# Linear attention, SwiGLU and two LayerNorms on 8 cores: x tiles loaded one step earlier, and a second pair of staging buffers for the int32 weights

## The chip, the cores and the metric

The kernel runs on all 8 cores of one Trainium2 chip. The batch of 16 sequences is split, two to a core, and the cores do not talk to each other. The time is that of the slowest core, in microseconds (us), from the first to the last instruction of the launch with what lies around it.

## The reference

With x of 16 x 2048 x 1024 in float32, layer 0 is

```python
q = elu(x @ Wq.T) + 1          # 16 heads of 64
k = elu(x @ Wk.T) + 1
v = x @ Wv.T
KV  = einsum('bshd,bshe->bhde', k, v)          # one 64 x 64 matrix per head and sequence
out = einsum('bshd,bhde->bshe', q, KV)
out = out / (einsum('bshd,bhd->bsh', q, k.sum(axis=1)) + 1e-6)
x = layernorm(x + out @ Wo.T)
h = silu(x @ (w_gate/127).T) * (x @ (w_up/127).T)      # hidden 3072, int32 weights
x = layernorm(x + h @ (w_down/127).T)
```

## The kernel before

**Two phases of attention.** A core holds 2 sequences of 2048 tokens. Since KV needs all tokens of a sequence, `phase1` goes first over the 16 token tiles of 128: it computes k and v of a tile (lines 535 and 549, 16 matmuls each), then the per-head products of the tile before (`emit_kv`, line 484), which VectorE adds up in `kv_acc`. Then 4 tiles of 512 tokens follow, each with a `phase2` (q, attention output, Wo, LayerNorm 1) and a `phase3` (gate and up projections, 24 slabs `m` of 128 hidden units, lines 1112 and 1125, with `silu` on ScalarE, line 1144, and the product into `h_fm` on VectorE, line 1152). The down projection (line 718) of a 512-token tile is done within `phase2` of the next one. The order of the tiles in `phase1` starts at tile 4 and ends with tiles 0 to 3, so that `xT` then holds the first 512 tokens for `phase2`.

**How x comes in.** `load_x_ld` (line 439) loads 128 tokens in float32 into one of two buffers `x_f32`, `load_x_cast` (line 448) turns them into bf16 on ScalarE, and `load_x_tp` (line 457) transposes them by DMA into a quarter of `xT`. In `phase1` all three for tile u+1 are in the body of tile u: load and cast at its head, the transpose at its end. `phase2` does the same for the next 512 tokens of the same sequence in the steps of `px`; for the last 512 tokens of a sequence (`next_x` is None) it does nothing, and the first tile of the next sequence is loaded at the head of the next `phase1`.

**Weights.** In the first sequence they come in while the work runs: Wk and Wv directly (`load_pair_direct`, through four staging buffers, of which two are the `x_f32` buffers), then, four jobs per tile of `phase1` (`drain_w_jobs`), Wq and Wo in float32 (cast on ScalarE, line 383, written back to HBM as bf16), and the 24 slabs of w_down in int32 (cast on VectorE and GpSimd into `wd_buf`). The gate and up slabs are loaded by `load_slab`. In the first `phase3` of the kernel (`first_tile`) each is an int32 image of 512 KB, loaded into a staging buffer `stg_i32` (line 1021), cast into `wgu[:, gi, m % 4, :]` (line 1033: gate on VectorE, up on GpSimd) and written to a bf16 copy in HBM (line 1048) that all later tiles read (lines 1062 and 1070). Slab m+4 is asked for in the body of slab m. Gate images always go through `outb[:, 0]` and up images through `outb[:, 1]`. The gate cast is emitted one slab later (`defer_vec`), ahead of that slab's `h_fm` on VectorE.

**What sets the order.** There is no scheduler: each engine executes its instructions in the order of the Python code. All DMAs, loads, stores and transposes alike, are issued by SyncE (SP) in that one order, each with its waits ahead of it; a `Track` for each buffer gives the waits (the readers and the writer before). So one DMA that waits holds back all behind it.

Of the kernel before, what the change touches and what calls it, by code (L numbers as in the profile page):

```python
# [9 lines left out]
I32 = mybir.dt.int32  # L10
# [4 lines left out]
SEQ = 2048  # L15
NSEQ = 2
D = 1024
# [165 lines left out]
def build_program(n_seq=NSEQ, n_tiles=NTILE // NSEQ, stop_after=None):  # L183
# [17 lines left out]
    with contextlib.ExitStack() as ctx:  # L201
# [75 lines left out]
        tr_silu = [Track() for _ in range(2)]  # L277
        tr_stgi = [Track() for _ in range(4)]
        tr_stgb = [Track() for _ in range(4)]
# [11 lines left out]
        for r in range(2):  # L291
# [4 lines left out]
                   wgu[:, 0, :, :].rearrange("p a b -> p (a b)").bitcast(I32)[:, 0:D],  # L296
                   wgu[:, 1, :, :].rearrange("p a b -> p (a b)").bitcast(I32)[:, 0:D]]
        stg_bf = [h_fm[:, 2 * i:2 * i + 2, :].rearrange("p a b -> p (a b)")
# [145 lines left out]
        def load_x_cast(ent, tq):  # L444
            ld, xr = ent
            ct = P.op("scalar",
                      lambda e, xr=xr, tq=tq:
                      e.activation(x_bf[:, tq, :], x_f32[:, xr, :], AF.Copy),  # L448
                      waits=[ld, tr_xbf[tq].begin_write()])
            tr_x[xr].add_reader(ct)  # L450
            tr_xbf[tq].end_write(ct)
            return ct
# [17 lines left out]

        def phase1(s, first):
            NCH = SEQ // 128
            pend = {}

            def emit_kv(u):
# [23 lines left out]
                else:  # L499
# [8 lines left out]
            order = [(u + CPT) % NCH for u in range(NCH)]  # L508
            cts = {0: load_x_cast(load_x_ld(s * SEQ + order[0] * 128),
                                  order[0] % CPT)}  # L510
            load_x_tp(cts.pop(0), order[0] % CPT)
            if first:
                load_pair_direct("wk", "wv")
            for u in range(NCH):
                if u + 1 < NCH:
                    cts[u + 1] = load_x_cast(
                        load_x_ld(s * SEQ + order[u + 1] * 128),
                        order[u + 1] % CPT)
                tq = order[u] % CPT
# [9 lines left out]
                for j in range(NJ):  # L529
                    for hl in range(2):  # L530
# [10 lines left out]
                            inc=last)  # L541
                bend(kbk, tok)
                for j in range(NJ):
                    for hl in range(2):
# [47 lines left out]
                pend[u] = (kr, kvr, t_k, t_v)  # L592
                if u + 1 < NCH:
                    load_x_tp(cts.pop(u + 1), order[u + 1] % CPT)

# [414 lines left out]
        def load_slab(m, first_tile=False, both_gp=False, defer_vec=None):  # L1010
# [4 lines left out]
            if first_tile:  # L1015
                for gi, (mat, img) in enumerate((("wg", wi_imgs["wgi"]),
                                                 ("wu", wi_imgs["wui"]))):
                    sl = (2 * m + gi) % 2
                    ld = P.dma(f"w3i{sl}",
                               lambda sy, img=img, m=m, sl=sl:  # L1020
                               sy.dma_start(stg_i32[sl], img[m]),
                               waits=[tr_stgi[sl].begin_write(),
                                      tr_outb[sl].begin_write()],
                               eng=BULKQ)
                    tr_stgi[sl].end_write(ld)
                    tr_outb[sl].end_write(ld)

                    def mk_ct(gi=gi, r=r, sl=sl, ld=ld, m=m, mat=mat,
                              both_gp=both_gp):
                        eng = "gpsimd" if (both_gp or gi == 1) else "vector"  # L1030
# [6 lines left out]
                        tr_stgi[sl].add_reader(ct)  # L1037
                        tr_outb[sl].add_reader(ct)
                        tr_wgu[gi][r].end_write(ct)
# [130 lines left out]
        for s in range(n_seq):  # L1170
            phase1(s, first=(s == 0))
            if stop_after == "P1":
# [5 lines left out]
            for g in range(n_tiles):  # L1178
                tidx = s * n_tiles + g
                sl3 = CPT - 1 + (tidx % 2)  # L1180
                nx = (s * SEQ + (g + 1) * TILE) if g + 1 < n_tiles else None
                fj = None
# [78 lines left out]
```

How the kernel before makes its waits and increments, by code:

```python
        def closure(eng, fn=fn, real_waits=real_waits, tok=tok, sem=sem):  # L128
            for s, v in real_waits:
                eng.wait_ge(s, v)
            inst = fn(eng)
            if tok is not None:
                inst.then_inc(sem, 1)
# [15 lines left out]
        def closure(e, fn=fn, real_waits=real_waits, sem=sem):  # L149
            for s, v in real_waits:
                e.wait_ge(s, v)
            fn(e).then_inc(sem, 16)
# [7 lines left out]
        def closure(eng, real_waits=real_waits):  # L160
            for s, v in real_waits:
                eng.wait_ge(s, v)
```

## Time and profile before

| | |
|---|---|
| median of the runs, us | 1936.92 |
| the runs, us | 1872.54 and 2001.31 |
| the profiled execution's own time, us | 1867.76 |
| its span on the slowest core (core 1), us | 1866.2 |
| spans of the 8 cores, us | 1850.5 to 1866.2 |
| TensorE busy, us (share of the span) | 1570.0 (84%) |
| ScalarE, VectorE busy, us | 545.9, 519.3 |
| bytes moved by DMA in core 1 | 255.28 MB, mean 137 GB/s |

All rows below are of the profiled execution, core 1; times in them count from the start of its span. The first sequence ends at 968 us. Engines: PE is TensorE, ACT ScalarE, DVE VectorE, POOL GpSimd, SPq the issue of a DMA by SyncE. A busy time of PE can overlap the start of the next group by a few tenths of a microsecond. In the windows view, the DMA share is the time that DMA packets took, as a share of 16 engines; packets that overlap can take it over 1.

### The profile page before, as it was taken

The numbers are of one execution on the slowest core, as the hardware profiler recorded it, in microseconds if no ns is written. First come the engines' busy times: TensorE is split into PE (matmuls) and PEld (weight loads), VectorE is DVE, ScalarE is ACT, GpSimd is POOL, SyncE is SP. The second block draws the span as 40 slices with busy tenths as digits, with TensorE's granted clock in tenths as the row PEclk, the third lists the DMA queues.
The fourth block names the chain that finished last, engine by engine and source line by source line (L and its number), as shares of the span: only waits on it lengthen the run. The fifth ranks groups of instructions, "written<-read, shape, count | busy, mean of one in ns | idle before, by whom it ended". The sixth has DMA issues, their size and how long they took to land.

```text
span 1866.2 us, 23063 instructions; the slowest of 8 cores (1850.5 to 1866.2 us)
## 1 busy us (share of the span) xinstructions
PE 1570.0 (84%) x7424; PEld 686.1 (37%) x7424; DVE 519.3 (28%) x979; ACT 545.9 (29%) x801; POOL 42.6 (2%) x44
## 2 busy tenths in 40 slices
PE   2677755766999899989888888899899999989998
PEld 0233322322444344434333333344344344434443
DVE  1142342123321332232113333312331332233111
ACT  2432213111342152224113331432252234114213
POOL 0010001110000000000000000000000000000000
PEclk9798977989999999999899998899899999999999
DMA  7999447885444245413653433355145334512431
GB/s 230 250 300 261 119 132 178 252 250 169 113 130 153 63 108 156 138 29 96 204 152 88 99 73 114 91 153 147 47 120 163 101 95 134 154 53 68 138 106 45
DMA packets 213236, 255.28 MB, mean 137 GB/s; under 512 B 136320, under 2 KB 136320, under 8 KB 212096
## 3 DMA queue, kind: packets, MB, share of 16 engines
q1 hardware_dynamic: 213120, 253.81, 47.9%
q8 instruction: 64, 1.05, 0.2%
q14 instruction: 52, 0.43, 0.1%
HBM read 184.55 MB, written 37.75 MB: 119 GB/s over the span
## 4 chain that ended last, share of the span: by engine, by line
PE 67%; DMA 13%; DVE 8%; ACT 6%; issue 4%; SPq 1%; DVEq 0%; ACTq 0%; POOL 0%; POOLq 0%
PE ps_c L718 18%; PE ps_a L1112 16%; PE ps_b L1125 15%; PE ps_b L924 5%; DMA outb<-wgi 5%; PE ps_a L535 3%; PE ps_b L549 2%; PE ps_a L549 2%; PE ps_b L535 2%; DVE t L812 2%; ACT texp L819 2%; DVE q_fm L826 2%; PE ps_a L799 2%; DMA res<-wo 1%; DMA x_f<-wv 1%
## 5 line engine op out<-in xcount | busy, mean ns | idle before, releaser
L1125 PE MATMUL ps_b<-ln1T,wgu 128*128 128x512 bf16 x1536 | 372.5, 386 | 32.3 <-DVE h_fm L1152 32.3
L1112 PE MATMUL ps_a<-ln1T,wgu 128*128 128x512 bf16 x1536 | 368.6, 383 | 26.9 <-DMA ln1T<-ln_bf 9.4
L718 PE MATMUL ps_c<-wd_buf,h_fm 128*128 128x512 bf16 x1536 | 355.7, 392 | 0.0
L1144 ACT ACTIVATE silu_b<-ps_a,consts 128x512 bf16<-128x512 f32 x192 | 131.1, 687 | 538.9 <-PE ps_a L1112 460.3
L1152 DVE SCALAR_TENSOR_TENSOR h_fm<-ps_b,silu_b 128x512 bf16<-128x512 f32 x192 | 131.9, 691 | 487.6 <-PE ps_b L1125 454.6
L1125 PEld LDWEIGHTS ps_b<-ln1T,wgu 128*128 128x128 bf16 x1536 | 151.3, 99 | 223.6 <-issue 51.0
L1112 PEld LDWEIGHTS ps_a<-ln1T,wgu 128*128 128x128 bf16 x1536 | 151.2, 99 | 215.3 <-issue 40.0
L718 PEld LDWEIGHTS ps_c<-wd_buf,h_fm 128*128 128x128 bf16 x1536 | 153.5, 101 | 186.9 <-issue 21.4
L924 PE MATMUL ps_b<-wpair,attnT 128*128 128x512 bf16 x512 | 134.1, 422 | 30.3 <-DVE res L948 16.7
L622 ACT ACTIVATE texp<-res 128x1024 bf16<-128x1024 f32 x64 | 67.3, 1051 | 299.7 <-DVE res L741 238.1
L799 PE MATMUL ps_a<-xT,wpair 128*128 128x512 bf16 x512 | 126.3, 396 | 31.9 <-DVE q_fm L826 27.0
L535 PE MATMUL ps_a<-wpair,xT 128*128 128x512 bf16 x256 | 70.3, 430 | 70.9 <-ACT wpair L413 34.5
L535 PE MATMUL ps_b<-wpair,xT 128*128 128x512 bf16 x256 | 64.4, 409 | 34.8 <-ACT v_tm L572 19.4
L924 PEld LDWEIGHTS ps_b<-wpair,attnT 128*128 128x128 bf16 x512 | 53.0, 107 | 101.5 <-issue 59.2
L799 PEld LDWEIGHTS ps_a<-xT,wpair 128*128 128x128 bf16 x512 | 48.5, 100 | 108.2 <-issue 62.6
L819 ACT ACTIVATE texp<-t 128x512 bf16<-128x512 bf16 x64 | 40.3, 629 | 124.1 <-DVE t L812 124.0
L847 PE MATMUL ps_a<-kvbd,q_fm 128*128 128x130 bf16 x256 | 29.3, 237 | 48.9 <-DVE attn_bf L889 30.4
L448 ACT ACTIVATE x_bf<-x_f 128x1024 bf16<-128x1024 f32 x56 | 57.9, 1043 | 26.9 <-DMA x_f<-x 26.9
L535 PEld LDWEIGHTS ps_a<-wpair,xT 128*128 128x128 bf16 x256 | 25.4, 105 | 109.6 <-issue 89.5
L826 DVE SCALAR_TENSOR_TENSOR q_fm<-ps_a,texp 128x512 bf16<-128x512 f32 x64 | 44.3, 692 | 64.0 <-ACT texp L819 64.0
L741 DVE SCALAR_TENSOR_TENSOR res<-ps_c,ln_bf 128x1024 f32<-128x1024 f32 x32 | 39.0, 1219 | 82.8 <-PE ps_c L718 79.9
L549 PE MATMUL ps_b<-wpair,xT 128*128 128x512 bf16 x256 | 58.8, 383 | 0.6
(59 smaller groups left out, 800.8 us busy)
## 6 DMA issues: line engine op xcount, KB each, us to landing
wgu<-scr_wg SPq DMA_DIRECT2D x168, 256.0 KB, 2.7
wgu<-scr_wu SPq DMA_DIRECT2D x168, 256.0 KB, 2.6
x_f<-x SPq DMA_DIRECT2D x56, 512.0 KB, 4.1
out<-outb SPq DMA_DIRECT2D x32, 512.0 KB, 2.7
outb<-wgi SPq DMA_DIRECT2D x24, 512.0 KB, 5.0
outb<-wui SPq DMA_DIRECT2D x24, 512.0 KB, 5.3
outb<-wdi SPq DMA_DIRECT2D x12, 512.0 KB, 7.6
wgu<-wdi SPq DMA_DIRECT2D x12, 512.0 KB, 8.6
```

The costliest lines, as they stand in the source:

```text
L535: t.matmul(kps[:, hl * 512:(hl + 1) * 512], xT[:, j, tq * 128:(tq + 1) * 128], wpair[:, 0, j, hl * 512:(hl + 1) * 512], start=(j == 0), st ...
L549: t.matmul(vps[:, hl * 512:(hl + 1) * 512], xT[:, j, tq * 128:(tq + 1) * 128], wpair[:, 1, j, hl * 512:(hl + 1) * 512], start=(j == 0), st ...
L622: e.activation(texp[:], res[:, rr, :], AF.Square, accum_out=stats[:, sl, 1:2]),
L718: t.matmul(d_view[:, pr, hl * 512:(hl + 1) * 512], h_fm[:, hm, sc * 128:(sc + 1) * 128], wd_buf[:, hm, hl * 512:(hl + 1) * 512], start=(hm ...
L799: t.matmul(ps_a[:, (i % 2) * 512:(i % 2 + 1) * 512], wpair[:, 0, j, i * 128:(i + 1) * 128], xT[:, j, :], start=(j == 0), stop=(j == NJ - 1)),
L819: lambda e: e.activation(texp[:, 0:TILE], t1[:, 0:TILE], AF.Exp),
L826: v.scalar_tensor_tensor(q_fm[:, i, :], ps_a[:, (i % 2) * 512:(i % 2 + 1) * 512], 0.0, texp[:, 0:TILE], ALU.max, ALU.add),
L924: t.matmul(ps_b[:, hl * 512:(hl + 1) * 512], attnT[:, tc, e_, :], wpair[:, 1, e_, hl * 512:(hl + 1) * 512], start=(e_ == 0), stop=(e_ == N ...
L1112: t.matmul(ps_a[:, (m % 2) * 512:(m % 2 + 1) * 512], wgu[:, 0, r, j * 128:(j + 1) * 128], ln1T[:, j, :], start=(j == 0), stop=(j == NJ - 1)),
L1125: t.matmul(ps_b[:, (m % 2) * 512:(m % 2 + 1) * 512], wgu[:, 1, r, j * 128:(j + 1) * 128], ln1T[:, j, :], start=(j == 0), stop=(j == NJ - 1)),
L1144: e.activation(silu_b[:, m % 2, :], ps_a[:, (m % 2) * 512:(m % 2 + 1) * 512], AF.Silu, scale=consts[:, 2:3]),
L1152: v.scalar_tensor_tensor(h_fm[:, m, :], ps_b[:, (m % 2) * 512:(m % 2 + 1) * 512], INV127, silu_b[:, m % 2, :], ALU.mult, ALU.mult),
```

## The change

Three things are changed.

1. `phase1` loads x two tiles ahead. The loads of tiles 0 and 1 stand at its head, the load of tile u+2 and the transpose of tile u+1 stand between the k and v matmuls of tile u, and the cast of tile u+1 stays at the head of tile u.
2. `phase2` of the last 512 tokens of the first sequence loads, casts and transposes tiles 4 to 7 of the second sequence (the first four in the order of `phase1`), and `phase1` of the second sequence then starts its loads at the fifth.
3. In the first `phase3`, slabs with odd m from 5 on are staged in `attnT` (two halves, for gate and up) instead of `outb`. `attnT` is idle in `phase3`.

```diff
@@ phase1
-            cts = {0: load_x_cast(load_x_ld(s * SEQ + order[0] * 128),
-                                  order[0] % CPT)}
-            load_x_tp(cts.pop(0), order[0] % CPT)
+            start_i = 4 if pre_x else 0
+            cts = {}
+            lds = {}
+
+            def p1_ld(i):
+                if start_i <= i < NCH:
+                    lds[i] = load_x_ld(s * SEQ + order[i] * 128)
+
+            def p1_cast(i):
+                if i in lds:
+                    cts[i] = load_x_cast(lds.pop(i), order[i] % CPT)
+
+            def p1_tp(i):
+                if i in cts:
+                    load_x_tp(cts.pop(i), order[i] % CPT)
+
+            p1_ld(0)
+            p1_ld(1)
+            p1_cast(0)
+            p1_tp(0)
             if first:
+                p1_cast(1)
                 load_pair_direct("wk", "wv")
             for u in range(NCH):
-                if u + 1 < NCH:
-                    cts[u + 1] = load_x_cast(
-                        load_x_ld(s * SEQ + order[u + 1] * 128),
-                        order[u + 1] % CPT)
+                p1_cast(u + 1)
...
                 bend(kbk, tok)
+                p1_ld(u + 2)
+                p1_tp(u + 1)
...
-                if u + 1 < NCH:
-                    load_x_tp(cts.pop(u + 1), order[u + 1] % CPT)
@@ load_slab
-                    sl = (2 * m + gi) % 2
+                    sl = gi + (4 if (m >= 4 and m % 2 == 1) else 0)
+                    if sl >= 4:
+                        alias = [tr_attnT[(sl - 4) * 2], tr_attnT[(sl - 4) * 2 + 1]]
+                    else:
+                        alias = [tr_outb[sl]]
                     ld = P.dma(f"w3i{sl}",
                                lambda sy, img=img, m=m, sl=sl:
                                sy.dma_start(stg_i32[sl], img[m]),
-                               waits=[tr_stgi[sl].begin_write(),
-                                      tr_outb[sl].begin_write()],
+                               waits=[tr_stgi[sl].begin_write()]
+                                     + [t.begin_write() for t in alias],
                                eng=BULKQ)
@@ the calls
-            phase1(s, first=(s == 0))
+            phase1(s, first=(s == 0), pre_x=(s > 0))
...
-                nx = (s * SEQ + (g + 1) * TILE) if g + 1 < n_tiles else None
+                if g + 1 < n_tiles:
+                    nx = s * SEQ + (g + 1) * TILE
+                elif s + 1 < n_seq:
+                    nx = (s + 1) * SEQ + CPT * 128
+                else:
+                    nx = None
```

**SP in the first `phase3`.** These are the first rows of the queue of SyncE there before the change: `wgi` and `wui` are the int32 images of gate and up, `scr_wg` and `scr_wu` their bf16 copies in HBM; a semaphore in brackets is what a row waits for.

```order
L1021 DMA outb<-wgi 128x1024 [waits sem_gpsimd,dsl_w3i0]
L1021 DMA outb<-wui 128x1024 [waits sem_gpsimd,dsl_w3i1]
L1048 DMA scr_wg<-wgu 128x1024 [waits dsl_scw0]
L1048 DMA scr_wu<-wgu 128x1024 [waits dsl_scw1]
L1021 DMA outb<-wgi 128x1024 [waits sem_vector,dsl_w3i0]
L1021 DMA outb<-wui 128x1024 [waits sem_gpsimd,dsl_w3i1]
L1048 DMA scr_wu<-wgu 128x1024 [waits dsl_scw1]
L1048 DMA scr_wg<-wgu 128x1024 [waits dsl_scw0]
L1021 DMA outb<-wgi 128x1024 [waits sem_vector,dsl_w3i0]
L1021 DMA outb<-wui 128x1024 [waits sem_gpsimd,dsl_w3i1]
```

And the same place after the change:

```order
L1042 DMA outb<-wgi 128x1024 [waits sem_gpsimd,dsl_w3i0]
L1042 DMA outb<-wui 128x1024 [waits sem_gpsimd,dsl_w3i1]
L1071 DMA scr_wg<-wgu 128x1024 [waits dsl_scw0]
L1071 DMA scr_wu<-wgu 128x1024 [waits dsl_scw1]
L1042 DMA attnT<-wgi 128x1024 [waits sem_tensor]
L1042 DMA attnT<-wui 128x1024 [waits sem_tensor,dsl_at0,dsl_at1]
L1071 DMA scr_wu<-wgu 128x1024 [waits sem_gpsimd,dsl_scw1]
L1071 DMA scr_wg<-wgu 128x1024 [waits sem_vector,dsl_scw0]
L1042 DMA outb<-wgi 128x1024 [waits dsl_w3i0]
L1042 DMA outb<-wui 128x1024 [waits dsl_w3i1]
```

Before, the load of each slab waited for the casts of the slab just ahead of it (`sem_vector`, `sem_gpsimd`), and the stores of that slab came behind. Now the loads of two slabs stand ahead of the stores that wait for the casts of the first of them, and a load itself waits for no cast that its queue has not already passed.

**SP from the last `phase3` of the first sequence into the second `phase1`.** The first two rows are the last gate and up slabs loaded in advance for the next tile; then come the x tiles of the second sequence. Before:

```order
L1062 DMA wgu<-scr_wg 128x1024 [waits sem_tensor,dsl_wg1]
L1070 DMA wgu<-scr_wu 128x1024 [waits sem_tensor,dsl_wu1]
L439 DMA x_f<-x 128x1024 [waits dsl_x0]
L457 DMA_TRANSPOSE xT<-x_bf 128x8x128 [waits sem_scalar,dsl_xt0]
L439 DMA x_f<-x 128x1024 [waits dsl_x1]
L457 DMA_TRANSPOSE xT<-x_bf 128x8x128 [waits sem_scalar,dsl_xt1]
```

After:

```order
L1085 DMA wgu<-scr_wg 128x1024 [waits sem_tensor,dsl_wg1]
L1093 DMA wgu<-scr_wu 128x1024 [waits sem_tensor,dsl_wu1]
L441 DMA x_f<-x 128x1024 [waits dsl_x0]
L441 DMA x_f<-x 128x1024 [waits dsl_x1]
L459 DMA_TRANSPOSE xT<-x_bf 128x8x128 [waits sem_tensor,sem_scalar,dsl_xt0]
L441 DMA x_f<-x 128x1024 [waits dsl_x0]
```

The first transpose here was that of the sequence's first tile in the order of `phase1`; now it is that of its fifth, and the first four stand some 50 rows further up, in `phase2`.

**SP in the first `phase1`.** One tile of x among the loads of w_down (`wdi`), before:

```order
L457 DMA_TRANSPOSE xT<-x_bf 128x8x128 [waits sem_tensor,sem_scalar,dsl_xt1]
L439 DMA x_f<-x 128x1024 [waits dsl_x0]
L342 DMA outb<-wdi 128x1024 [waits sem_vector,dsl_wi0]
L342 DMA outb<-wdi 128x1024 [waits sem_gpsimd,dsl_wi1]
L342 DMA wgu<-wdi 128x1024 [waits sem_vector,dsl_wi2]
L342 DMA wgu<-wdi 128x1024 [waits sem_gpsimd,dsl_wi3]
```

After:

```order
L441 DMA x_f<-x 128x1024 [waits dsl_x0]
L459 DMA_TRANSPOSE xT<-x_bf 128x8x128 [waits sem_tensor,sem_scalar,dsl_xt1]
L344 DMA outb<-wdi 128x1024 [waits sem_vector,dsl_wi0]
L344 DMA outb<-wdi 128x1024 [waits sem_gpsimd,dsl_wi1]
L344 DMA wgu<-wdi 128x1024 [waits sem_vector,dsl_wi2]
L344 DMA wgu<-wdi 128x1024 [waits sem_gpsimd,dsl_wi3]
```

The load of the tile after next now stands ahead of the transpose instead of behind it; the four weight loads keep their place.

## Rows read from the trace of the kernel before

**Rows 1.** The page: busy shares in 40 slices of the span.
```profile
PE   2677755766999899989888888899899999989998
DMA  7999447885444245413653433355145334512431
```

**Rows 2.** Timeline of PE, around the first phase3 and the one after it.
```profile
312.57 3.57 PE L1112 MATMUL ps_a<-ln1T,wgu 128*128 128x512 bf16 x8 [9.37 <-DMA ln1T<-ln_bf]
...
443.12 3.62 PE L799 MATMUL ps_a<-xT,wpair 128*128 128x512 bf16 x16
...
529.86 1.89 PE L1112 MATMUL ps_a<-ln1T,wgu 128*128 128x512 bf16 x8
...
614.16 3.62 PE L799 MATMUL ps_a<-xT,wpair 128*128 128x512 bf16 x16
```

**Rows 3.** Waits in the first phase3, 313 to 443 us: waiter <- releaser, total, times, longest.
```profile
DVE wgu L1033 <- DMA outb<-wgi: 89.5, 19, 6.6
PE ps_b L1125 <- DVE h_fm L1152: 32.3, 15, 4.3
```

**Rows 4.** Timeline of SP and DVE in the first phase3.
```profile
313.34 0.46 SPq L1021 DMA_DIRECT2D outb<-wgi  x1
...
351.25 0.33 SPq L1021 DMA_DIRECT2D outb<-wgi  x1
...
357.24 0.69 DVE L1033 CAST wgu<-outb 128x1024 bf16<-128x1024 int32 x1 [5.52 <-DMA outb<-wgi]
358.07 0.33 SPq L1021 DMA_DIRECT2D outb<-wgi  x1
...
435.83 0.69 DVE L1033 CAST wgu<-outb 128x1024 bf16<-128x1024 int32 x1 [3.27 <-DMA outb<-wgi]
```

**Rows 5.** Windows: per stretch busy times, granted clock, DMA share, GB/s.
```profile
core 1: us, PE busy (x) PEld busy (x) DVE busy (x) ACT busy (x) POOL busy (x), PEclk, DMA share, GB/s
0.00:17.00 17.00, 0.00 (x0) 0.00 (x0) 0.27 (x5) 3.40 (x3) 0.20 (x4) 1.00 0.50 120
42.00:54.00 12.00, 5.00 (x18) 1.86 (x16) 1.58 (x2) 6.41 (x7) 0.00 (x0) 0.88 0.86 261
54.00:101.00 47.00, 29.06 (x144) 11.79 (x144) 9.17 (x9) 20.87 (x21) 0.00 (x0) 0.79 0.94 256
112.00:165.00 53.00, 45.69 (x269) 19.98 (x270) 24.33 (x27) 17.37 (x17) 10.97 (x10) 0.97 1.09 314
313.34:435.83 122.49, 90.18 (x352) 36.18 (x351) 25.35 (x40) 16.40 (x23) 19.98 (x19) 0.89 0.84 252
886.00:896.00 10.00, 1.85 (x9) 0.64 (x7) 0.69 (x1) 0.69 (x1) 0.00 (x0) 0.74 0.96 350
```

**Rows 6.** Timeline of PE and SP from the first sequence into the second.
```profile
968.57 0.36 SPq L439 DMA_DIRECT2D x_f<-x  x1
...
976.63 5.06 PE L535 MATMUL ps_a<-wpair,xT 128*128 128x512 bf16 x16 [8.62 <-DMA xT<-x_bf]
981.53 3.62 PE L549 MATMUL ps_b<-wpair,xT 128*128 128x512 bf16 x16
```

**Rows 7.** Timeline of PE: phase2 of the fourth 512 tokens, its first group and the one behind it.
```profile
785.77 3.62 PE L799 MATMUL ps_a<-xT,wpair 128*128 128x512 bf16 x16
...
872.45 1.89 PE L1112 MATMUL ps_a<-ln1T,wgu 128*128 128x512 bf16 x8
```

**Rows 8.** The xT tile in the first 235 us, and SP and PE in the first phase1.
```profile
  DMA xT<-x_bf: 19.3, 5
...
7.72 1.33 SPq L457 DMA_TRANSPOSE xT<-x_bf  x1
...
40.04 0.33 SPq L439 DMA_DIRECT2D x_f<-x  x1
...
161.87 8.70 SPq L457 DMA_TRANSPOSE xT<-x_bf  x1
...
175.58 6.21 PE L535 MATMUL ps_b<-wpair,xT 128*128 128x512 bf16 x16 [9.29 <-DMA xT<-x_bf]
```

More of the change, by code:

```diff
@@ L277, in build_program @@
         tr_silu = [Track() for _ in range(2)]
-        tr_stgi = [Track() for _ in range(4)]
+        tr_stgi = [Track() for _ in range(6)]
         tr_stgb = [Track() for _ in range(4)]
@@ L296, in build_program @@
                    wgu[:, 0, :, :].rearrange("p a b -> p (a b)").bitcast(I32)[:, 0:D],
-                   wgu[:, 1, :, :].rearrange("p a b -> p (a b)").bitcast(I32)[:, 0:D]]
+                   wgu[:, 1, :, :].rearrange("p a b -> p (a b)").bitcast(I32)[:, 0:D],
+                   attnT[:, 0:2, :, :].rearrange("p a b c -> p (a b c)").bitcast(I32),
+                   attnT[:, 2:4, :, :].rearrange("p a b c -> p (a b c)").bitcast(I32)]
         stg_bf = [h_fm[:, 2 * i:2 * i + 2, :].rearrange("p a b -> p (a b)")
@@ L469, in dbg_dump, with phase1 @@
             P.sync_wait([tk])
-        def phase1(s, first):
+        def phase1(s, first, pre_x=False):
             NCH = SEQ // 128
@@ L1021, in load_slab @@
                                sy.dma_start(stg_i32[sl], img[m]),
-                               waits=[tr_stgi[sl].begin_write(),
-                                      tr_outb[sl].begin_write()],
+                               waits=[tr_stgi[sl].begin_write()]
+                                     + [t.begin_write() for t in alias],
                                eng=BULKQ)
                     tr_stgi[sl].end_write(ld)
-                    tr_outb[sl].end_write(ld)
+                    for t in alias:
+                        t.end_write(ld)
                     def mk_ct(gi=gi, r=r, sl=sl, ld=ld, m=m, mat=mat,
-                              both_gp=both_gp):
+                              both_gp=both_gp, alias=alias):
                         eng = "gpsimd" if (both_gp or gi == 1) else "vector"
@@ L1037, in mk_ct @@
                         tr_stgi[sl].add_reader(ct)
-                        tr_outb[sl].add_reader(ct)
+                        for t in alias:
+                            t.add_reader(ct)
                         tr_wgu[gi][r].end_write(ct)
```

## The prediction

> **What bounds the kernel now.** I read the slices of the page first [rows 1]. The reader is to see three kinds of stretch: in the first four slices TensorE is busy 2 to 7 tenths while the DMA engines are at 7 to 9; in slices 7 and 8 (counting from 0, 326 to 420 us) TensorE is at 6 and 7 and DMA at 8; from slice 10 on TensorE is at 8 and 9 nearly everywhere and DMA at half or less. So TensorE is the bound outside the first 445 us, and there only a stall of its own can be won; before that the DMAs are.
>
> The second view is the timeline of TensorE, which gives each stage its length [rows 2]. The first `phase3` runs from 312.57 to 443.12 us, 130.6 us; the next one does the same matmuls in 614.16 - 529.86 = 84.3 us, 3.5 us a slab. The difference of 46 us is what the int32 slabs cost. The third view, the waits of that stretch, tells how [rows 3]: VectorE waits 89.5 us in 19 waits for gate images to land, and since its queue is in order the product `h_fm` stands behind that cast; TensorE then waits 32.3 us for `h_fm`. The timeline shows the cycle [rows 4]: the load issued at 351.25 us is cast at 357.24, 6.0 us later, and only then, at 358.07, is the next load issued, because there is one staging buffer for gate images. The windows view says that this leaves DMA at 252 GB/s and a share of 0.84 [rows 5].
>
> The last stall that the change speaks of is at the seam of the two sequences [rows 6]: x is asked for only at 968.57 us, and TensorE, done with `phase3`, stands still for 8.62 us.
>
> **Part 1: the staging buffers.** In the changed queue of SP the loads of slab m+1 are out before the casts of slab m are waited for, so two slabs are in flight. A load at the head then waits for no cast that SP hasn't passed, and nothing new is queued behind a wait: the store of the up slab, which now is what SP stands at, was behind such a wait before. The two casts need slab m-4's matmuls to be done, which TensorE, slowed to the DMA's pace, is. The buffer `attnT` was read last by the Wo matmuls before 312 us, so its first load finds it free.
>
> The stretch then ends with the stream of bytes. From the first gate load at 313.34 to the landing of the last at 435.83 us are 122.5 us [rows 4]. In the queue up to that landing are 20 gate and 19 up images of 0.524 MB (20.45 MB) and 38 stores of 0.262 MB (9.96 MB), 30.4 MB. Bounds for the rate, with these bytes:
> - 256 GB/s, as between 54 and 101 us, where loads, stores and transposes are mixed and the share is 0.94 [rows 5]: 118.8 us
> - 314 GB/s, as between 112 and 165 us, mostly int32 loads, share 1.09 [rows 5]: 96.8 us
> - between them the stretch itself, 252 GB/s at a share of 0.84, which is 300 GB/s at 1.00 [rows 5]: 101.3 us.
>
> I take 300, as it is the same mixture of packets, and add 1.5 us for the landing of the last image, my estimate: an image takes 6.0 us now from issue to cast, of which it and the up image beside it are 3.5 us at 300 GB/s, and a part of the rest is paid each time. The part gives 122.5 - 102.8 = 19.7 us, with bounds of 2.2 and 24.2. TensorE does not become the bound: its 24 slabs at 3.5 us end at 397 us, the stream at 416. The 7.3 us from the last gate cast to the end of the stage (435.83 to 443.12) stay. Later tiles only move up: their x is there already, and their slabs are read from the copies in HBM.
>
> **Part 2: the seam.** Four tiles of x lie in `xT` before TensorE is done with `phase3`. The 8.62 us go, and with them the slow restart: the 16 matmuls behind the stall took 5.06 us against 3.62 for the same number right after [rows 6], 1.4 us. What is late next is the PSUM bank that `silu` of slab 23 reads, and that is free before TensorE arrives. 10.1 us are won. The fifth tile has the time of four others, 7.2 us of matmuls each, to come in, and is no stall. The lower bound is 8.6 us, if the restart stays slow.
>
> The price is four loads, four casts on ScalarE and four transposes more in the last `phase2` of the sequence, and behind the last two of these transposes stand an output store and the load of Wk and Wv. The `phase2` of the second 512 tokens carries just this and shows the price [rows 2, 7]: it takes 529.86 - 443.12 = 86.7 us, the last one, without it, 872.45 - 785.77 = 86.7 us. I take nothing. What hides it is the down projection of the last 128 tokens on TensorE; without that cover the Wk and Wv load would slip by the two transposes.
>
> **Part 3: the first `phase1`.** TensorE waits here for x transposes 5 times, 19.3 us in all, 9.29 of them at once at 175.58 us [rows 8], where the transpose is queued behind two stores of 2 MB. As DMA is full from 112 to 165 us, the end of that wait is set by the bytes ahead of it. The changed order puts one tile of x more (0.524 MB, 1.7 us at 300 GB/s) ahead of each transpose. In return tile 1 is loaded at the very start, where SP stands still until 7.72 us and DMA is half idle [rows 5, 8], instead of at 40.04 us: 1.7 us fewer from there on. The two cancel. What is left is idle DMA time that earlier loads may fill: 0.14 of 12 us (42 to 54 us) and 0.06 of 47 us (54 to 101 us) [rows 5], 1.7 + 2.8 = 4.5 us, since ScalarE then finds x there and comes to its weight casts sooner. I take half of it, 2.3 us won. The bounds are 6.2 us won (all of it, and the 1.7 of the start without its counterweight) and 8.5 us lost (1.7 us on each of the 5 waits). In the second `phase1` DMA has room, and swapping load and transpose costs nothing there.
>
> **The sum.** 19.7 + 10.1 + 2.3 = 32.1 us. Against the profiled execution's own time, 1867.8 us, that is 1836 us, a ratio of 0.983. The two runs shown are 1872.54 and 2001.31 us and their median, 1936.92, is only their mean; the forecast is on the scale of the lower one, which it would put at 1841.
>
> **Rivals.**
> - **The stream is not held back by buffers.** The DMA engines might already do all that this mixture of loads and stores allows. For it: 256 GB/s at 54 to 101 us is no more than the 252 of the stage [rows 5]. Against it: the share there is 0.94 and here 0.84, and transposes take part of it there. Part 1 gives 2.2 us or less, the sum is 14.6, the time 1853.
> - **The stream runs faster than 314 GB/s.** For it: between 886 and 896 us 350 GB/s flow [rows 5]. Against it: these are bf16 loads alone. At 350 the 30.4 MB take 86.9 us, 88.4 with the landing; TensorE, at 397 us, is still done earlier. Part 1 gives 34.1 us, the sum is 46.5, the time 1821. The Trainium skill, "HBM Reference", Specifications, says that each of two cores that stream at once gets about 358 GB/s; the 350 GB/s above agree, and no stretch with stores comes near. By that rule the bytes would take 84.9 us and part 1 would give 36 us, a time of about 1819.
> - **The earlier x loads fill the queue in front of the transposes (the other side).** At 161.87 us the issue of one transpose took 8.70 us, where the first took 1.33, with 4 MB of stores just ahead of it [rows 8]; SP and all that it feeds stand still meanwhile. If one more tile of x ahead of it did the same to a transpose among the w_down loads, each would cost 8.70 - 1.33 = 7.4 us. It decides from five of them on: 36.9 us against the 32.1 won, 1873 us, slower than before. Against it: of the 19.3 us that TensorE waits for x, 9.29 stand behind this one transpose, so none of the others, which have 2.6 MB of w_down and x before them, was held back as much.
>
> **How the numbers follow.** My forecast holds with a chance of 0.60, for itself from 1827 (a rate of 314 and all 6.2 us of part 3) to 1850 (a rate of 275, where part 1 gives 10.5 us, and 3 us lost in part 3). The fast stream has 0.18, the stream without gain 0.17, the full queue 0.05. The range of 8 in 10 goes from 1817 to 1866 us: below it takes in the fast stream, above it the case without gain with part 3 at its bad end (1867.8 - 2.2 - 10.1 + 8.5 = 1864). A measurement of this kernel can tell about 2% from no change, 37 us, so "faster by over 2%" is below 1830: the fast stream nearly whole, 0.16, and the quick edge of the forecast, 0.11, together 0.27. Slower by over 2% takes the full queue with more transposes than five, 0.02. Within 2% is the rest, 0.71.
>
> **What would show it.** Right: in the first `phase3` the gate loads on average 5.1 to 5.4 us apart (101 us over 19) instead of 6.4 (122.5 over 19), at 300 GB/s and a share near 1, the stage at 108 to 114 us in place of 130.6, and VectorE's waits for gate images still the largest but near 65 us. At the seam no wait of TensorE for `xT`, and its first 16 k matmuls at 3.6 us. In the first `phase1` the end of the long wait within 3 us of 175.6. Wrong: a rate that stays at 252 GB/s with two slabs in flight; a stall that comes back at the fifth tile of the second sequence; a TensorE wait for `ln1T` or for Wk and Wv in the last tile of the first sequence longer than before; issues of transposes above 3 us between 105 and 153 us.

## The result and the profile after

The changed kernel takes 1834.9 us, the median of 11 runs (1833.6 to 1931.4). In some runs, such as that of 1931.4 us, one half of the chip has a lower granted clock and the time is longer; all ratios here leave such runs out on both sides. The ratio to the kernel before is 0.9798, with a 95% interval of 0.9752 to 0.9844. Measured again beside the experiments below (e5) it was 0.9826 (0.9804 to 0.9849). The forecast was 1836 us and 0.983. The profiled execution took 1841.2 us, 26.6 less than the 1867.8 of the one before; the measured ratios stand for 32 to 38 us.

The timeline of TensorE in the changed kernel, core 1 again, the first matmuls of each stage, answers to [rows 2, 6, 7]. Columns: start in us, length in us, line, output<-inputs, shape, and in brackets the wait ahead of it.

```profile
313.23 3.57 PE L1135 MATMUL ps_a<-ln1T,wgu 128*128 128x512 bf16 x8 [9.45 <-DMA ln1T<-ln_bf]
...
426.87 3.62 PE L816 MATMUL ps_a<-xT,wpair 128*128 128x512 bf16 x16
...
513.56 1.89 PE L1135 MATMUL ps_a<-ln1T,wgu 128*128 128x512 bf16 x8
...
881.39 3.52 PE L1135 MATMUL ps_a<-ln1T,wgu 128*128 128x512 bf16 x8 [9.58 <-DMA wgu<-scr_wg]
...
952.09 3.62 PE L552 MATMUL ps_a<-wpair,xT 128*128 128x512 bf16 x16
955.55 3.62 PE L568 MATMUL ps_b<-wpair,xT 128*128 128x512 bf16 x16
```

The reader is to see three things. The first `phase3` lasts 426.87 - 313.23 = 113.6 us, where it was 130.6 [rows 2]. The `phase2` behind it is unchanged, 86.7 us. And at 952.09 us the second sequence starts without a bracket: no wait for x, and the 16 matmuls take 3.62 us instead of 5.06 [rows 6]. What is left between the sequences is the row at 881.39, a wait of 9.58 us for slab 4, which was there before (8.7 us) and which the change does not touch.

The waits of that first `phase3`, 313 to 427 us, answer to [rows 3] (waiter <- releaser, total, times, longest):

```profile
DVE wgu L1055 <- DMA attnT<-wgi: 36.3, 10, 5.8
...
DVE wgu L1055 <- DMA outb<-wgi: 31.4, 8, 5.5
PE ps_b L1148 <- DVE h_fm L1175: 21.2, 14, 3.5
```

VectorE still waits for gate images, 67.7 us in all, now for both buffers in turn; it was 89.5. TensorE's wait for `h_fm` fell from 32.3 to 21.2 us. The queue of SP in that stage answers to [rows 4]:

```profile
313.92 0.47 SPq L1042 DMA_DIRECT2D outb<-wgi  x1
...
350.64 0.40 SPq L1042 DMA_DIRECT2D attnT<-wgi  x1
...
354.67 0.33 SPq L1071 DMA_DIRECT2D scr_wu<-wgu  x1
355.15 0.33 SPq L1071 DMA_DIRECT2D scr_wg<-wgu  x1
355.58 0.39 SPq L1042 DMA_DIRECT2D outb<-wgi  x1
...
413.70 0.38 SPq L1042 DMA_DIRECT2D attnT<-wgi  x1
```

The loads into `attnT` at 350.64 and into `outb` at 355.58 are 4.9 us apart; the first was cast at 357.06:

```profile
357.06 0.69 DVE L1055 CAST wgu<-attnT 128x1024 bf16<-128x1024 int32 x1 [3.26 <-DMA attnT<-wgi]
```

So the second load went out 1.5 us before the first was used; before the change it had to go out after. Over the stage the gate loads are (413.70 - 313.92) / 19 = 5.25 us apart. The windows view of the stretch answers to the row of 313 to 436 us in [rows 5] (columns as there):

```profile
0.00:17.00 17.00, 0.00 (x0) 0.00 (x0) 0.27 (x5) 3.96 (x4) 0.20 (x4) 1.00 0.53 137
...
42.00:54.00 12.00, 7.00 (x18) 2.39 (x18) 1.84 (x2) 5.22 (x6) 0.00 (x0) 0.91 0.79 233
54.00:101.00 47.00, 29.12 (x144) 11.77 (x144) 9.17 (x9) 22.10 (x23) 0.00 (x0) 0.79 1.00 258
...
313.34:417.00 103.66, 83.55 (x344) 34.29 (x342) 25.00 (x39) 15.72 (x22) 18.72 (x18) 0.93 0.91 294
```

In the first `phase3` the DMA share rose from 0.84 to 0.91 and the rate from 252 to 294 GB/s. In the first `phase1` there is little to see: in the first 17 us the rate rose from 120 to 137 GB/s, from 42 to 54 us it fell from 261 to 233, and from 54 to 101 us the share rose from 0.94 to 1.00 while the rate went only from 256 to 258 GB/s. What TensorE waits for there has changed its name. The view of the tile `xT`, first 235 us, before:

```profile
  ACT v_tm L572: 27.8, 10
  DMA xT<-x_bf: 19.3, 5
```

and after:

```profile
  DMA xT<-x_bf: 32.3, 7
  ACT v_tm L591: 7.3, 7
  ACT texp L598: 5.8, 1
```

Before, 47.1 us of waits for ScalarE and transposes together; after, 45.4. TensorE now waits little for ScalarE and waits for the transpose instead; e3 and e8 below show that the order of the x loads does this.

### The profile page after: what moved, and what is told of

The parts are those of the page before. It is cut to its first block, busy times and chain, and to the rows that moved or that the text cites. A ratio compares the mean times of both kernels' runs of the same rounds, so it can differ in the third digit from the quotient of the medians.

```text
span 1839.6 us, 23066 instructions; the slowest of 8 cores (1815.7 to 1839.6 us)
## 1 busy us (share of the span) xinstructions
PE 1563.3 (85%) x7424; PEld 684.5 (37%) x7424; DVE 520.8 (28%) x979; ACT 544.9 (30%) x801; POOL 41.8 (2%) x44
## 4 chain that ended last, share of the span: by engine, by line
PE 67%; DMA 13%; DVE 7%; ACT 7%; issue 4%; SPq 1%; POOL 1%; DVEq 0%; ACTq 0%; POOLq 0%
PE ps_c L735 18%; PE ps_a L1135 16%; PE ps_b L1148 15%; PE ps_b L941 5%; PE ps_a L568 3%; PE ps_a L552 3%; PE ps_b L552 2%; PE ps_b L568 2%; DVE t L829 2%; ACT texp L836 2%; DMA attnT<-wui 2%; DVE q_fm L843 2%; DMA xT<-x_bf 2%; PE ps_a L816 2%; DMA scr_wu<-wgu 1%
## 5 line engine op out<-in xcount | busy, mean ns | idle before, releaser
L1148 PE MATMUL ps_b<-ln1T,wgu 128*128 128x512 bf16 x1536 | 367.7, 383 | 21.2 <-DVE h_fm L1175 21.2
L1167 ACT ACTIVATE silu_b<-ps_a,consts 128x512 bf16<-128x512 f32 x192 | 131.2, 687 | 522.2 <-PE ps_a L1135 464.6
L864 PE MATMUL ps_a<-kvbd,q_fm 128*128 128x130 bf16 x256 | 28.9, 235 | 48.9 <-DVE attn_bf L906 30.4
L504 DVE TENSOR_TENSOR kv_acc<-kv_acc,ps_c 128x520 f32<-128x520 f32 x30 | 20.9, 696 | 135.9 <-PE ps_c L486 135.9
```

The costliest lines, as they stand in the source:

```text
L1148: t.matmul(ps_b[:, (m % 2) * 512:(m % 2 + 1) * 512], wgu[:, 1, r, j * 128:(j + 1) * 128], ln1T[:, j, :], start=(j == 0), stop=(j == NJ - 1)),
L1167: e.activation(silu_b[:, m % 2, :], ps_a[:, (m % 2) * 512:(m % 2 + 1) * 512], AF.Silu, scale=consts[:, 2:3]),
```

## The experiments

Since the 8 cores of one execution differ by some microseconds, I compare stages by the median over the cores of one profiled execution: for each core, the time from the first matmul of the stage to the first of the next. The stages are the first `phase1`, the first `phase3`, the last `phase3` of the first sequence (it takes in the waits for slab 4 and, before the change, for x at the seam) and the second `phase1`. Ratios are to the kernel before, measured beside each set, with 95% intervals. The two without a ratio were run once each and are read from their profile alone; part of their result is not computed.

| kernel | ratio | phase1, 1st | phase3, 1st | phase3 at the seam | phase1, 2nd |
|---|---|---|---|---|---|
| before | 1 | 209.4 | 131.2 | 102.5 | 157.6 |
| the change | 0.9798 (0.9752 to 0.9844) | 209.1 | 112.6 | 94.7 | 155.9 |
| e1 staging only | 0.9898 (0.9872 to 0.9923) | 210.5 | 108.6 | 102.3 | 157.6 |
| e2 seam only | 0.9937 (0.9916 to 0.9959) | 208.4 | 130.5 | 94.1 | 155.9 |
| e3 order of x only | 0.9995 (0.9981 to 1.0009) | 208.1 | 129.6 | 104.3 | 157.5 |
| e4 staging and seam | 0.9839 (0.9819 to 0.9858) | 210.5 | 110.0 | 93.6 | 155.7 |
| e5 the change again | 0.9826 (0.9804 to 0.9849) | 205.5 | 108.7 | 92.8 | 155.6 |
| e6 three slabs in flight | 0.9811 (0.9794 to 0.9828) | 206.3 | 107.6 | 93.0 | 155.9 |
| e7 Wk and Wv in pieces | 0.9771 (0.9752 to 0.9789) | 207.4 | 108.4 | 84.6 | 154.8 |
| e8 transpose first | 0.9820 (0.9798 to 0.9842) | 206.1 | 111.0 | 94.1 | 155.9 |
| e9 no stores | one run, 1810.7 us | 206.9 | 85.2 | 93.9 | 156.1 |
| e10 no stores, one pair | one run, 1837.2 us | 207.6 | 114.2 | 94.6 | 156.2 |
| e11 e6 and e7 together | 0.9785 (0.9755 to 0.9815) | 207.0 | 106.0 | 84.6 | 154.7 |

### One part at a time

The first set takes the change apart. Staging alone:

```diff
-                    sl = (2 * m + gi) % 2
+                    sl = gi + (4 if (m >= 4 and m % 2 == 1) else 0)
...
-                               waits=[tr_stgi[sl].begin_write(),
-                                      tr_outb[sl].begin_write()],
+                               waits=[tr_stgi[sl].begin_write()]
+                                     + [t.begin_write() for t in alias],
```

> Only the staging of odd slabs in attnT is changed; x is loaded as before. Theory A (the parts add, each with the size seen on TensorE's timeline of core 1: 16.9 us for the first phase3, 9 to 10 for the seam, nothing for the order of the x loads): ratio to before 0.991, first phase3 113 to 115 us instead of 130.6, seam stall of 8.6 us still there. Theory B (the staging is worth more than core 1 shows, since all cores give the HBM back sooner and the other cores gain more): ratio 0.985 or lower. A rival of both, that the DMA engines had no room and the gain came from elsewhere: first phase3 128 us or more, ratio 0.998 or higher.

Measured: 0.9898 (0.9872 to 0.9923), 19 us on 1868. The wait for x at the seam is still there (9.8 us on its slowest core). The ratio is that of theory A, and its interval does not reach the 0.985 of theory B. The stage is not: 108.6 us, where theory A said 113 to 115. Over the cores it became 22.6 us shorter than before, more than core 1 had shown (16.9), so that much of theory B's argument stands. The third theory, that the gain came from elsewhere, falls.

The seam alone, with the order of `phase1` as before:

```diff
-            phase1(s, first=(s == 0))
+            phase1(s, first=(s == 0), pre_x=(s > 0))
...
+                elif s + 1 < n_seq:
+                    nx = (s + 1) * SEQ + CPT * 128
```

> Only the four x tiles of the second sequence are loaded in the last phase2 of the first; the order of loads and transposes in phase1 and the staging are as before. Theory A: ratio 0.995 (9 to 10 us), no wait of TensorE for xT at the seam, the last phase2 at 86.7 us within 0.6. Rival (the seam only moves the wait to the fifth tile, or the load of Wk and Wv slips by the two transposes): ratio 0.998 or higher, a wait of 3 us or more at the fifth tile, or one for wgu longer than 8.7 us by 2 or more.

Measured: 0.9937, 11.8 us. The timeline of TensorE at the seam on its slowest core shows no wait in front of the k matmuls of line 551:

```profile
965.91 1.89 PE L1146 MATMUL ps_b<-ln1T,wgu 128*128 128x512 bf16 x8
967.64 3.62 PE L551 MATMUL ps_a<-wpair,xT 128*128 128x512 bf16 x16
```

The wait for slab 4 is 9.43 us on that core, and between cores it differs much: 5.6 to 9.4 us here (median 7.2), 5.5 to 10.2 in the kernel before (median 6.8). So no slip of the Wk and Wv load can be seen. The rival falls.

The order of the x loads alone:

```diff
+            p1_ld(0)
+            p1_ld(1)
...
                 bend(kbk, tok)
+                p1_ld(u + 2)
+                p1_tp(u + 1)
```

> Only the x loads of phase1 are moved (load of tile u+2 ahead of the transpose of tile u+1, tile 1 loaded at the start). Theory A: ratio 1.000 within 0.001; the long wait for xT ends within 3 us of 175.6 us; TensorE's waits for xT grow and those for v_tm on ScalarE shrink by about as much. The prediction's part 3 (idle DMA time is filled): ratio 0.999, 2.3 us won. Rival (this part carries the 10 us by which the measured ratio beats the profiles): ratio 0.995 or lower. The other side: each transpose later by a tile's bytes, 1.002 to 1.005.

Measured: 0.9995 (0.9981 to 1.0009). It is no change that can be measured, neither a gain of 10 us nor the other side; the 2.3 us of the prediction (0.999) lie inside the interval too. The waits moved as expected: for `xT` 30.2 us, for `v_tm` 6.3. The long wait for `xT` ended at 173.84 us.

The two parts that do something, with the order of the x loads taken back from the change:

```diff
-                p1_ld(u + 2)
-                p1_tp(u + 1)
...
+                p1_ld(u + 1)
                 p1_cast(u + 1)
...
                 pend[u] = (kr, kvr, t_k, t_v)
+                p1_tp(u + 1)
```

> The whole change without the new order in phase1: staging and seam. Theory A: the same as the whole change within 0.001, and the sum of the first two runs. If the order of the x loads costs what the later start of the second phase1 tiles in the profile suggests (0.7 to 2.4 us), this one is faster than the whole change by 0.0005 to 0.0015. Rival (the order carries part of the gain): slower than the whole change by 0.003 or more.

Measured: 0.9839 (0.9819 to 0.9858). The sum of the first two, 1 - 0.0102 - 0.0063 = 0.9835, is the same: the parts add. Against the first 0.9798 of the whole this left 0.004 open, so the whole was run again (no edit):

> The whole change once more, with the runs of before on the same chip as the three that follow. The first set gave staging 0.9898, seam 0.9937, order 0.9995, staging and seam 0.9839; the first measurement of the whole gave 0.9798 (0.9752 to 0.9844). Theory A (the parts add): 0.983 to 0.984, so that the first value was the spread of the runs of before. Theory C (the order of the x loads is worth 0.004 beside the other two parts, though nothing alone): 0.980.

Measured: 0.9826 (0.9804 to 0.9849). That is within 0.0004 of theory A: the three parts, 0.0102 + 0.0063 + 0.0005, make 0.0170, and the whole gives 0.0174. The 0.9798 rests on runs of before that spread from 1864.9 to 1891.5 us, and its wide interval takes in 0.983.

### What holds the stream of weights

e6 adds a third pair of staging buffers and lets four stores wait instead of two, so that a third slab is asked for before SP stands at a store.

```diff
+                   q_fm[:, 0:4, :].rearrange("p a b -> p (a b)").bitcast(I32),
+                   q_fm[:, 4:8, :].rearrange("p a b -> p (a b)").bitcast(I32)]
...
-                    sl = gi + (4 if (m >= 4 and m % 2 == 1) else 0)
+                    sl = gi + (0, 4, 6)[m % 3 if m >= 4 else 0]
...
-                        while len(slab_state["st"]) > 2:
+                        while len(slab_state["st"]) > 4:
```

> The whole change plus a third pair of staging buffers (in q_fm, idle there) and four pending stores instead of two, so that the loads of three slabs are out before SP waits for a cast. Theory A (at two slabs in flight the stream of 30 MB is held by the DMA engines: share 0.91, 294 GB/s): the first phase3 shrinks by 0 to 3 us from 113.6, the rate stays below 305 GB/s, ratio to before within 0.001 of the whole change. Rival (buffers still bind, the engines could do 314 GB/s or more): phase3 at 108 us or less, ratio 0.003 better than the whole change.

Measured: 0.9811 beside 0.9826, intervals that overlap, and a first `phase3` of 107.6 us beside 108.7. The windows view of its slowest core in that stage:

```profile
308.00:405.00 97.00, 81.26 (x344) 33.90 (x342) 25.15 (x39) 15.71 (x22) 18.72 (x18) 0.94 0.94 311
```

A share of 0.94 and 311 GB/s look like a rise from the 0.91 and 294 of the changed kernel, but these are single cores. The medians over the cores, each from its first gate load of the stage to its last gate cast, are 0.92 and 314 GB/s in e5 and 0.95 and 317 here, both above the 305 I had given as the most. What is left to win by buffers is about 1 us. The rival of 108 us or less with a ratio better by 0.003 is met in the stage and missed in the ratio (0.0015); the stage had been at 108.7 already, so the step, not the level, decides, and it is small.

Two runs then separate the buffers from the bytes. They leave out the 48 stores of the bf16 copies; SP waits for the same casts in their place, and later tiles read other copies of the same size.

```diff
-                            st = P.dma(f"scw{(2 * m + gi) % 2}",
-                                       lambda sy, mat=mat, m=m, gi=gi, r=r:
-                                       sy.dma_start(scr[mat][m], wgu[:, gi, r, :]),
-                                       waits=[ct], eng=BULKQ)
+                            P.sync_wait([ct])
...
-                       sy.dma_start(wgu[:, 0, r, :], scr["wg"][m]),
+                       sy.dma_start(wgu[:, 0, r, :], scr_qkvo["wq"][:, (m % 8) * D:(m % 8 + 1) * D]),
```

> The whole change without the 48 stores of the bf16 copies of gate and up (12.6 MB); SP still waits for the same casts in the same places, and the later tiles read the bf16 copies of Wq and Wo instead, the same number of bytes, so that part of the result is not computed. Theory A (the first phase3 lasts as long as its stream of loads and stores at about 300 GB/s): the 20.4 MB of loads alone take 68 us, TensorE's 24 slabs at 3.5 us take 84, so the stage falls to 85 to 95 us, median over the cores, from 110. Rival (two slabs in flight are held by the time from issue to cast, whatever the bytes): 105 us or more.

Measured: first `phase3` 85.2 us, as theory A had it and one microsecond above the 84.3 of a later one. With a third of the bytes gone, TensorE is the bound. The window of that stage on the slowest core:

```profile
310.00:395.00 85.00, 84.63 (x380) 38.13 (x386) 29.52 (x44) 17.77 (x25) 20.80 (x20) 0.98 0.81 272
```

TensorE is busy in 84.63 of 85 us. Leaving out the stores takes away more than bytes: a cast into a slot of `wgu` also waits for the store of the slab that lay there. But that store is four slabs old, some 21 us in the changed kernel, and the stores of that stage land 4.5 to 4.7 us after their issue (median), so this wait is long over. The other run has, on top, the one pair of buffers:

```diff
-                    sl = gi + (4 if (m >= 4 and m % 2 == 1) else 0)
+                    sl = gi
```

> The same without stores, and with the one pair of staging buffers of the kernel before; part of the result is not computed. Theory A (one pair is held by issue to cast): the load of the next slab still waits for the cast of the last, so a slab takes the fixed part of a load plus the bytes of an image pair, 4 to 5 us instead of 6.4: stage 100 to 118 us, clearly longer than with two pairs. Rival (only the bytes ever mattered): the same as with two pairs, 85 to 95 us.

Measured: 114.2 us, with the same few bytes. The timeline of SP in that kernel shows the old cycle, two gate loads in a row:

```profile
344.59 0.33 SPq L1042 DMA_DIRECT2D outb<-wgi  x1
...
350.10 0.33 SPq L1042 DMA_DIRECT2D outb<-wgi  x1
```

and that of VectorE the cast between them:

```profile
349.28 0.69 DVE L1055 CAST wgu<-outb 128x1024 bf16<-128x1024 int32 x1 [4.22 <-DMA outb<-wgi]
```

The load of 344.59 is cast 4.7 us later and the next goes out at 350.10. The DMA engines are far from full meanwhile: from the first gate load to the last gate cast the share is 0.61, at 195 GB/s (medians over the cores). The four corners of this stage are thus: one pair with stores 131.2 us, one pair without 114.2, two pairs with stores 110.0 (mean of the medians of the change, e1, e4 and e5: 112.6, 108.6, 110.0, 108.7), two pairs without 85.2. With one pair the time from issue to cast is the bound and the stores lengthen it; with two, the bytes are, at a share of 0.92 rather than 1.

### The order in the queue of the first phase1

```diff
-                p1_ld(u + 2)
                 p1_tp(u + 1)
+                p1_ld(u + 2)
```

> The whole change, but with the transpose of tile u+1 ahead of the load of tile u+2 again; tile 1 is still loaded at the start. Tests the working of part 3 of the prediction. If one tile of x more ahead of each transpose costs 1.7 us and the early load of tile 1 gives 1.7 back, the long wait for xT in the first phase1 now ends 1.7 us sooner than in the changed kernel (near 176 instead of 178 us), and the kernel is 1 to 2 us faster, at the edge of what shows. Rival (the order in the queue does not matter, since the load is asked for while SP would stand at the transpose anyway): same end of the wait within 0.5 us, TensorE's waits for xT still near 32 us in the first phase1.

Measured: 0.9820 beside 0.9826, and a first `phase1` of 206.1 us beside 205.5. The long wait ended at 171.08 us on its slowest core and at 174.92 on that of e5, but these are different cores, and between the cores of one execution this stage differs by 4 to 11 us. The medians over the cores say more. The long wait ends at 169.2 us here, and at 169.5, 168.4 and 170.1 in e5, e6 and e7, which were measured beside it with the new order: no 1.7 us are seen, though so small a shift could hide. What did change is the kind of wait: for `xT` 18.4 us here against 28 to 31 in those three, for `v_tm` 23.0 against 6 to 9. In the kernel before they were 18.7 and 28.5. So it is the place of the load, ahead of the transpose or behind it, that decides whether TensorE waits for the transpose or for ScalarE, and in time the two come to the same. Neither expectation holds whole: the end of the wait is that of the rival, its 32 us of waits for `xT` are not.

### A version that beats both

In the changed kernel the largest wait of TensorE left in the second half of the first sequence is the 9.58 us for slab 4. SP shows what is ahead of it:

```profile
863.07 0.38 SPq L426 DMA_DIRECT2D wpair<-scr_wk  x1
863.60 0.61 SPq L426 DMA_DIRECT2D wpair<-scr_wv  x1
864.35 0.35 SPq L1085 DMA_DIRECT2D wgu<-scr_wg  x1
```

Two DMAs of 2 MB each are issued just ahead of the 256 KB of slab 4, and that is needed at 871.8. e7 loads Wk and Wv in 16 pieces, one behind each slab:

```diff
-            if next_kv_pair:
-                load_pair("wk", "wv")
...
+                if kv_chunks:
+                    j_, si, mat = kv_chunks.pop(0)
+                    ld = P.dma(f"wp{(2 * j_ + si) % 4}",
+                               lambda sy, si=si, mat=mat, j_=j_:
+                               sy.dma_start(wpair[:, si, j_, :],
+                                            scr_qkvo[mat][:, j_ * D:(j_ + 1) * D]),
```

> The whole change, but Wk and Wv for the second sequence are loaded in 16 pieces of 256 KB, one behind the load of each slab of the last phase3 of the first sequence, instead of 4 MB in a row ahead of slab 4. In the changed kernel TensorE waits 9.6 us for slab 4 there. Expected: that wait goes and nothing takes its place, since a slab and a piece are 0.79 MB in 3.5 us, 228 GB/s: 9.5 to 11 us less than the whole change, ratio to before 0.978. Rival (the last pieces are late at the seam, or each piece delays a slab): a wait for wpair or for wgu of 3 us or more there, ratio 0.981 or higher.

Measured: 0.9771 (0.9752 to 0.9789), 1826.9 us, some 10 us less than the change beside it. The `phase3` at the seam falls to 84.6 us from 92.8, which is that of a tile without any wait, and the timeline there runs through slab 4 (the group at 869.73):

```profile
868.01 1.89 PE L1149 MATMUL ps_b<-ln1T,wgu 128*128 128x512 bf16 x8
869.73 1.89 PE L1136 MATMUL ps_a<-ln1T,wgu 128*128 128x512 bf16 x8
```

Both of its expectations hold, the time and the wait that goes. The two additions together:

> The whole change with Wk and Wv spread over the slabs and with three slabs in flight. If both add to the whole change as they did alone (0.9771 and 0.9811 against 0.9826): ratio to before 0.975 to 0.976, first phase3 107 to 108 us (median over the cores), last phase3 of the first sequence 84.6 us.

Measured: 0.9785 (0.9755 to 0.9815), where 0.975 to 0.976 was expected. Its two stages are as short as expected or shorter (106.0 and 84.6 us), but its runs went from 1819.6 to 1831.5 us, and it cannot be told from e7. That the additions add is not shown. e7, with the smaller edit and the narrow interval, is the version to keep.

## Why the prediction was right

**Part 1, the staging: the mechanism and the size are right, the working of the rate is not.** I had set 19.7 us for the step "the stretch ends with the stream of bytes", 30.4 MB at 300 GB/s. On core 1 it gave 16.9 us, by the medians of the change and of e5 18.6 and 22.5, and alone (e1) 0.0102, 19 us. On core 1 the way from the first gate load (313.92 us) to the last gate cast (420.15 us) took 106.2 us against my 102.8. I had scaled 252 GB/s at a share of 0.84 to 300 at 1.00. The share did not become full: it was 0.91 there, at which the same scaling gives 273 GB/s, and 294 flowed. Over the cores (medians) the change, e1, e4 and e5 reached 300 to 315 GB/s at shares of 0.92 to 0.94. So more bytes flowed for each busy microsecond of the DMA engines than before; why is open, and that 300 came out nearly right is in part luck. That the buffer was the cause is shown by e9 and e10: without stores the second pair is worth 29 us. The rival "the stream is not held back by buffers" fell. So did that of the fast stream: three slabs in flight reached 317 GB/s (median over the cores, 322 at most), not 350. The Trainium skill, "HBM Reference", Specifications, gives about 358 GB/s for each of two cores that stream at once. No core reached that with this mixture, and as a rate for this stream it would have put part 1, by the estimate in the prediction, at 36 us, where e1 gave 19.

**Part 2, the seam: right.** I had set 10.1 us, 8.62 for the wait and 1.4 for the slow restart. Both rows are gone in the trace. e2 gave 0.0063, 11.8 us (7.7 to 15.7). Its medians against those of before give 8.4 in the `phase3` and 1.7 in the second `phase1`, together 10.1, and some 1.1 us more in the `phase2` after it, which I had not seen (last section). The price of the extra loads in the last `phase2` was set at nothing. On core 1 the wait for slab 4 is 9.58 us where it was 8.73, but the medians over the cores are 6.8 us before and 7.2 in e2, 7.0 in e4, 5.9 in e5 and 7.8 in the first profile of the change, so no price can be told from the differences between cores.

**Part 3, the first phase1: the size cannot be told from nothing, and its working failed.** I had set 2.3 us won, as half of the idle DMA time. e3 alone gave 0.0005, 0.9 us (between 3.5 won and 1.7 lost). The stage takes 205.5 to 209.1 us in the eight kernels that have the new order as it is (mean of the medians 207.2) and 208.4 to 210.5 in the four that have the old one (before, e1, e2, e4; mean 209.7), 2.5 us; but most of the eight were measured in other sets than the four, and beside e1, e2 and e4 the new order alone (e3) has 208.1. The idle time was not filled as I had it: on core 1 the share fell from 0.86 to 0.79 in the first of the two stretches (42 to 54 us), and in the second (54 to 101 us) it rose to 1.00 with only 2 GB/s more. On core 1 of the changed kernel the long wait ended at 177.97 us instead of 175.58, which looks like a loss, but the medians over the cores are 172.7 and 172.9. That "the two cancel", a tile more ahead of each transpose against tile 1 at the start, agrees with this, but e8 did not show the first of the two. What I had left out are the waits for ScalarE, 27.8 us: the new order turned them into waits for transposes (e3, e8), so little was there to win.

**The other side** was a queue so full that transposes are slow to issue. Between 105 and 153 us none took over 1.6 us on core 1 of the changed kernel (2.1 on the others), and the one behind the 4 MB of stores took 7.29 where it had been 8.70. It fell.

**The sum.** Forecast 32.1 us; the three parts alone sum to 0.0170, 31.8 us, and the whole to 0.0174 in the second measurement, 32.5 us. That these agree to half a microsecond is luck: each of the intervals is 5 to 10 us wide, and the first measurement stands for 38 us.

## What to carry to other kernels

- A stage that loads, casts and reloads one staging buffer can run at the time from issue to cast; here a DMA share of 0.84 in such a stage was room. The gain of a second buffer can be estimated from the bytes of the stream, those of the stores in the same queue among them. The rate is the weak term: the share stopped at 0.92, and scaling the old rate by the share came near by luck.
- Test buffers and bytes as a 2 x 2: leave out the stores, add the buffers, do both. Either alone (114 or 110 us from 131) looks like the whole cause; together they are 46 us.
- A bulk load in one piece ahead of small loads that are due sooner can be a stall: 4 MB ahead of slab 4 held TensorE for 9.58 us on core 1. In 16 pieces between the slabs it cost next to nothing (84.6 us against 84.3).
- Before a small shift is read from one core, look at all of them: the first `phase1` differs by 4 to 11 us between the cores of one execution.

## What the runs showed that I had not expected

- The first `phase2` of the second sequence takes 84.2 us (median over the cores) in before and e1, and 82.8 to 83.1 in e2, e4, e5 and the changed kernel, though none of them touches it. The difference lies in one group, the last 16 matmuls of Wo, which stand behind a wait of some 3 us. On core 1 of e1 and of the changed kernel they are:

```profile
1168.18 6.34 PE L939 MATMUL ps_b<-wpair,attnT 128*128 128x512 bf16 x16 [3.34 <-DMA attnT<-attn_bf]
1175.52 4.96 PE L941 MATMUL ps_b<-wpair,attnT 128*128 128x512 bf16 x16 [2.99 <-DMA attnT<-attn_bf]
```

  The mean granted clock in them is 0.55 and 0.71 of the full one; on core 4 of the kernel before it is 1.00, and they take 3.61 us. The medians of their time over the cores are 6.3 to 6.4 us in before, e1 and e3, which keep the stall at the seam, and 4.9 to 5.1 in e2, e4, e5 and the changed kernel, which do not. So the gain is one of the granted clock; why the clock is down for a shorter part of that group is open.
- Stores of a third of the bytes, which nobody waits for at once, cost 17 us with one staging pair (114.2 to 131.2) and 25 with two (85.2 to 110.0), where TensorE sets the lower of the two times.
